# Three edits in one program: GpSimd's order and a subtraction in attention A, an addition in the dense stage, two clamps in attention B

## The reference

```python
x = x + attn_a(_layernorm(x))      # stage "attention A", with its own feed-forward network (first half of "dense")
x = x + ffn(_layernorm(x))         # per group of 1024 rows: two linear maps, no activation between them
x = x + attn_b(_layernorm(x))      # linear attention with memory, segments of 64 rows
x = x + ffn(_layernorm(x))
```

```python
# attn_a, for 16 heads of size 8 and 8 value groups r
score = softmax(einsum('bihd,bjhd->bhij', q, k))
out = einsum('bhij,bjrd->bihrd', score, v)
comp = softmax(concatenate([qv, out]) @ Ws.T + bs, axis=3)   # over r
out = (comp * out).sum(axis=3)
out = res + _lin(out, Wf, bf)                                # "y plus bias": res + bf
# attn_b
sigma(t) = elu(t) + 1       # = max(t, 0) + exp(min(t, 0)), taken of k and of q
```

## Time and profile before

| | us |
|---|---|
| median of 3 runs (1666.82 to 1677.94) | 1674.24 |
| the profiled execution | 1675.07 |
| its span, first to last instruction | 1673.3 |
| TensorE's mean granted clock | 0.962 of full speed |

### The profile page before, as it was taken

How to read it: one execution, slowest core, us unless ns; L and a number is a source line. 1 busy time by engine, 2 the same in 40 slices (tenths; PEclk the granted TensorE clock), 3 DMA queues, 4 the chain that set the end, 5 groups by cost and what they waited for, 6 DMA issues and landing times. The chain is left out here.

```text
span 1673.3 us, 46472 instructions
## 1 busy us (share of the span) xinstructions
PE 1459.9 (87%) x13668; PEld 1242.3 (74%) x13668; DVE 1220.1 (73%) x3362; ACT 869.2 (52%) x2019; POOL 902.9 (54%) x1308
## 2 busy tenths in 40 slices
PE   5899999999999999997587738999999999999986
PEld 3899889898889898897366526766676766667665
DVE  4378888888888888886245446888888888878774
ACT  2466666666666666665366623444444444444431
POOL 4456666666666666664588833444444444444431
PEclk9899999999999999999699958999999999999996
DMA  4423333233333232330444223333333333333330
GB/s 138 147 76 100 94 94 85 78 81 85 94 94 83 78 84 85 91 87 11 118 123 133 84 75 96 102 102 101 107 103 101 108 106 107 107 106 107 98 96 17
DMA packets 181695, 158.10 MB, mean 94 GB/s; under 512 B 12530, under 2 KB 163186, under 8 KB 181619
## 3 DMA queue, kind: packets, MB, share of 16 engines
q1 hardware_dynamic: 181618, 157.17, 32.9%
HBM read 113.09 MB, written 44.04 MB: 94 GB/s over the span
## 5 line engine op out<-in xcount | busy, mean ns | idle before, releaser
L597 PE MATMUL a_bank<-a_vp,a_prob 128*128 128x74 f32 x4096 | 603.6, 253 | 0.0
L597 PEld LDWEIGHTS a_bank<-a_vp,a_prob 128*128 128x128 f32 x4096 | 588.6, 192 | 7.5
L685 DVE TENSOR_REDUCE a_nmax<-a_bank 128x2 f32<-128x512 f32 x512 | 345.7, 681 | 142.9 <-PE a_bank L566 142.0
L484 ACT ACTIVATE a_prob<-a_bank 128x512 f32<-128x512 f32 x512 | 305.4, 596 | 245.8 <-PE a_bank L581 240.5
L581 PE MATMUL a_bank<-a_q_st,a_k_st 120*128 120x256 bf16 x1024 | 281.7, 276 | 27.6 <-POOL a_q_st L345 27.0
L566 PE MATMUL a_bank<-a_k_st,a_q_st 96*128 96x256 bf16 x1024 | 259.9, 277 | 16.9 <-DVE a_nmax L685 12.5
L1627 PE MATMUL c_o_bank<-c_vb,c_prob 128*128 128x96 f32 x1024 | 173.4, 293 | 17.9 <-DVE c_ad L1910 14.0
L1786 DVE TENSOR_REDUCE c_nmax<-c_bank 128x4 f32<-128x512 f32 x256 | 164.8, 684 | 19.7 <-PE c_bank L1597 17.2
L345 POOL TENSOR_SCALAR a_q_st<-a_mt 24x2048 bf16<-24x2048 bf16 x64 | 121.4, 1896 | 103.7 <-PE a_bank L581 60.8
L1492 ACT ACTIVATE c_prob<-c_bank 128x256 f32<-128x256 f32 x256 | 98.8, 386 | 145.8 <-PE c_bank L1577 144.2
L404 POOL TENSOR_TENSOR a_prod<-a_ov,a_wgt 128x512 f32<-128x512 f32 x128 | 151.3, 1182 | 37.3 <-POOL a_prod L404 17.1
(11 more groups left out here) (207 smaller groups left out, 2879.3 us busy)
## 6 DMA issues: line engine op xcount, KB each, us to landing
a_q_st<-scratch_a_parts_dram SPq DMA_DIRECT2D x64, 288.0 KB
a_k_st<-scratch_a_parts_dram SPq DMA_DIRECT2D x192, 96.0 KB
c_q_st<-scratch_c_parts_dram SPq DMA_DIRECT2D x64, 288.0 KB
c_k_st<-scratch_c_parts_dram SPq DMA_DIRECT2D x192, 96.0 KB
scratch_a_parts_dram<-a_parts SPq DMA_DIRECT2D x32, 384.0 KB, 2.7
scratch_c_parts_dram<-c_parts SPq DMA_DIRECT2D x32, 384.0 KB, 2.7
a_x<-in_x SPq DMA_DIRECT2D x32, 128.0 KB, 2.9
scratch_y<-a_y SPq DMA_DIRECT2D x32, 128.0 KB, 2.5
```

Of the source, the lines that this page charges most:

```text
L484: act.activation(prob[h % 4][:, :, :].rearrange("p a b -> p (a b)"), t_ps[h % 2][:, :], ACT.Exp).then_inc(exped, 1)
L597: mm = pe.matmul(o_ps[g % 2][:, at:at + VM], prob[h % 4][:, c, t * P:(t + 1) * P], vp[o][:, c, 0:VM], start=c == 0, stop=c == NT - 1)
L685: dve.tensor_reduce(nmax[:, t, 2 * g:2 * g + 2, 0], s_ps[t][:, :].rearrange("p (h k) -> p h k", h=2), AX.X, ALU.max, negate=True).then_inc ...
```

## The change

In attention A, GpSimd does norm instructions for r1 and the shift first, then the spread of half 0, then the four for r2. The subtraction `comp3 = comp2 - cmax` moves from VectorE's list to GpSimd's, behind the spread of half 1. In dense, y plus bias moves from GpSimd to VectorE, between the moments of x1 and the sum x2. In attention B the two clamps move from VectorE at step 1 to ScalarE at step 2, as Relu of x and Relu of -x; the exponential then takes -neg.

```diff
@@ attention_a, gpsimd body
                 if active(j, u, 2):
                     spread(1, n - 2, i)
+                if active(j, u, 3):
+                    b = n - 3
+                    pool.wait_ge(post, b * POST + 4)
+                    apart(pool, spare)
+                    pool.tensor_tensor(comp3[:, :, :], comp2[:, :, :],
+                                       cmax[:, :].unsqueeze(2).broadcast_to([P, H * NT, R]), ALU.subtract
+                                       ).then_inc(post, 1)
+                    pool.wait_ge(post, b * POST + 5)
...
                     norm(1, pool.tensor_scalar(rt[:, 0, :], mv[:, :, 1], EPS, None, ALU.add))
                     norm(2, pool.tensor_tensor(r1[:, :], rt[:, 0, :], half[:, :], ALU.pow))
-                    norm(3, pool.tensor_tensor(rt[:, 1, :], r1[:, :], r1[:, :], ALU.mult))
-                    norm(4, pool.tensor_tensor(rt[:, 2, :], rt[:, 1, :], mv[:, :, 1], ALU.mult))
-                    norm(5, pool.tensor_scalar(rt[:, 3, :], rt[:, 2, :], EPS, None, ALU.add))
-                    norm(6, pool.tensor_tensor(r2[:, :], rt[:, 3, :], half[:, :], ALU.pow))
-                    norm(7, pool.tensor_scalar(rt[:, 4, :], mv[:, :, 0], -1.0, None, ALU.mult))
-                    norm(8, pool.tensor_tensor(shift[:, :], rt[:, 4, :], r1[:, :], ALU.mult))
+                    norm(3, pool.tensor_scalar(rt[:, 4, :], mv[:, :, 0], -1.0, None, ALU.mult))
+                    norm(4, pool.tensor_tensor(shift[:, :], rt[:, 4, :], r1[:, :], ALU.mult))
                 if active(j, u, 1):
                     spread(0, n - 1, 1 - i)
+                if active(j, u, -1):
+                    apart(pool, spare)
+                    norm(5, pool.tensor_tensor(rt[:, 1, :], r1[:, :], r1[:, :], ALU.mult))
+                    norm(6, pool.tensor_tensor(rt[:, 2, :], rt[:, 1, :], mv[:, :, 1], ALU.mult))
+                    norm(7, pool.tensor_scalar(rt[:, 3, :], rt[:, 2, :], EPS, None, ALU.add))
+                    norm(8, pool.tensor_tensor(r2[:, :], rt[:, 3, :], half[:, :], ALU.pow))
@@ attention_a, vector
-                        lambda: dve.tensor_tensor(comp3[:, :, :], comp2[:, :, :], wide(cmax), ALU.subtract),
+                        None,
...
-                weighs(4, 5)
@@ dense, gpsimd body
-                if has(j, u, 0):
-                    pool.wait_ge(ay_in, (n + 1) * 32)
-                    if later(j, n, 2):
-                        pool.wait_ge(r_d, n - 1)
-                    pool.tensor_tensor(yb[i][:, :, :], y[i][:, :, :], rows(b_f), ALU.add).then_inc(yb_d, 1)
@@ dense, vector body, behind moments(1, n - 2, x1[i])
+                if has(j, u, 0):
+                    if isinstance(j, int) and n == 0:
+                        dve.wait_ge(loaded, N_LOAD * 16)
+                    dve.wait_ge(ay_in, (n + 1) * 32)
+                    if later(j, n, 2):
+                        dve.wait_ge(r_d, n - 1)
+                    dve.tensor_tensor(yb[i][:, :, :], y[i][:, :, :],
+                                      b_f[:, :].unsqueeze(1).broadcast_to([P, C, P]), ALU.add).then_inc(yb_d, 1)
@@ attention_b, scalar body
+                    if s == 2 and active(j, u, 0):
+                        if later(j, n, 1):
+                            act.wait_ge(sg_d, n)
+                        act.activation(flat(pos), ps_a[:, :], ACT.Relu).then_inc(pn_d, 1)
+                        act.activation(flat(neg), ps_a[:, :], ACT.Relu, scale=-1.0).then_inc(pn_d, 1)
...
-                        act.activation(nexp[:, :, :], neg[:, :, :], ACT.Exp).then_inc(nexp_d, 1)
+                        act.activation(nexp[:, :, :], neg[:, :, :], ACT.Exp, scale=-1.0).then_inc(nexp_d, 1)
@@ attention_b, vector body
-                    if s == 1 and active(j, u, 0):
-                        dve.wait_ge(kq_d, (n + 1) * 2)
-                        if later(j, n, 1):
-                            dve.wait_ge(sg_d, n)
-                        dve.tensor_scalar(flat(pos), ps_a[:, :], 0.0, None, ALU.max).then_inc(pn_d, 1)
-                        dve.tensor_scalar(flat(neg), ps_a[:, :], 0.0, None, ALU.min).then_inc(pn_d, 1)
```

More of the change, by code:

```diff
@@ L371, in body, with norm @@
                                                 ALU.subtract))
+                def norm(k, ins):
+                    ins.then_inc(norm_d, 1)
+                    pool.wait_ge(norm_d, (n + 1) * NORM + k)
+                    apart(pool, spare)
                 if active(j, u, -1):
@@ L377, in body @@
                         pool.wait_ge(z_d, (n + 1) * NT)
[L379 to L382, removed]
                     apart(pool, spare)
```

## The result

| | before | after |
|---|---|---|
| median of the runs of one chip, us | 1674.4 (20 runs, 1665.89 to 1679.26) | 1681.6 (20 runs, 1674.61 to 1686.28) |
| ratio, 95% interval | | 1.0044 [1.003, 1.0058] |
| span of the profiled execution, us | 1673.3 | 1679.6 |
| attention A, 31 rounds, us | 717.7 | 700.1 |
| dense, 15 rounds, us | 139.1 | 143.1 |

What follows compares the result with a forecast made beforehand. The prediction took TensorE's matmul order with short waits to bound both attentions, and a ScalarE-TensorE loop the dense stage. A -20, dense +6, B -16.5 made -30.5 from 1675.07: 1644 us, range 1611 to 1690.

Steps and rivals of the forecast that it cites:

- Attention B: Clamps moved to ScalarE: TensorE's waits for VectorE shrink, 0.55 us a block, 16.5 us gained over 30.
- given back: Rival: attention A's gain falls to 9 us and ScalarE's passes make an exponential in B late; 1672 us, chance 0.17.
- Attention A, spread between norm instructions: In attention A, the earlier lower-half spread removes TensorE's wait for it, 0.96 us a block.
- The subtraction: In attention A, moved to GpSimd's idle time, it removes TensorE's wait behind it: 0.25 us a block, bounds 0 and 0.66.
- The meeting: In attention A, later GpSimd products delay VectorE's two weighing steps; of 1.2 us a block 0.70 is left, 20 us.
- The slower rival, weighing meets spread: In attention A, the upper spread holds VectorE's second weighing step: 1.5 us a block more, 1708 us, chance 0.13.
- Dense: VectorE's moved addition holds the norm's first small GpSimd instruction, 0.4 us a unit, +6 us.
- The rival by GpSimd's load: GpSimd's load bounds the dense stage, so losing the addition gives -18 in place of +6: 1621 us, chance 0.08.

Runs made afterwards that it cites:

- only B: Kernel before with only the attention B edit, attention A and dense as before: ratio 1.0108.
- the whole change with the wait: Kernel after, plus GpSimd's addition sg in attention B waiting for VectorE's pair that normalizes z4: ratio 0.9789 to the kernel before, median 1638.98 us.
- only A: Kernel before with only the two attention A edits, dense and attention B as before: ratio 0.9883.
- only dense: Kernel before with only the dense edit, attention A and B as before: ratio 0.9998.

## Why the prediction was wrong

**Attention B is the step that failed**, and in it one thing: what comes behind VectorE's four steps on the maxima. Up to there it held: the cast stretched to 0.60 (forecast 0.5 to 0.7), the wait before the memory matmul gone, ScalarE's two passes 0.62 and 0.63 us and no exponential late, one table load in the page after too, and with the meeting taken away the round is 19.57 to 19.62 for a forecast of 19.6. The prediction summed TensorE's gain to the matmul at line 1698 and let all behind it move forward by the same 0.55. That matmul came as forecast, 0.71 us after GpSimd's last splitting part where it was 1.27. What lies behind it doesn't move together. Count from the end of GpSimd's last splitting part, which is fixed: 1211.12 before, 1202.97 after. The z4 pair starts at +1.75 before, behind VectorE's own list. After, it starts at +1.45, released by GpSimd's small instructions, which stand behind the splitting in GpSimd's list and so can't come earlier. The addition hangs on ScalarE's exponential of `neg`, and that on TensorE, whose wait in front had gone entirely: +2.51 before, +1.52 after. The pair needs 0.60. Before it was through at +2.35, with 0.16 us to spare; after, the addition starts 0.07 us behind the pair's start. The two rows (1212.87 to 1213.47 and 1213.63) were in the trace of before; the prediction names neither. Its rule for GpSimd, that a step moved on an engine may meet its neighbour, was applied in A and in dense, and for the cast in B, but not to what ScalarE's output releases. The price is -0.56 gained and +1.46 lost: +0.90 a round, 21.03 for 20.13.

That the time lies in the stated range is no merit. The rival nearest to it, "given back" (1672), had A's gain falling to 9 us and an exponential in B late; A kept 17.6, and no exponential was late.

The Trainium skill ("SBUF — State Buffer", section "SBUF: two separate sides") says that the SBUF ports which VectorE and GpSimd share are held by one of them for the whole instruction, whichever starts first, and that the other blocks fully. The trace agrees on the size: 1.42 us for the first of the pair is the addition's 1.27 and little more. It differs on who is first: VectorE's record starts at 1204.42, 0.07 us ahead of GpSimd's at 1204.49, and VectorE is the one that waits. The kernels after and "only B" show where the line runs between the records. In all 40 rounds in which GpSimd's starts 0.054 to 0.092 us behind VectorE's, the first of the pair is held (1.40 to 1.44 us). In all 6 in which it starts 0.101 to 0.186 us behind, the first takes 0.35, and only the second is held. One of the six, where the addition in its turn takes 1.36 for 1.27:

```profile
1058.24 1.55 DVE L1774 TENSOR_SCALAR c_z<-c_x,c_mv,c_rs 128x128 f32<-128x128 f32 x2 [0.18 <-POOL c_rs L1412]
```
```profile
1058.35 1.36 POOL L1458 TENSOR_TENSOR c_sg<-c_pos,c_nexp 128x512 f32<-128x512 f32 x1 [0.21 <-ACT c_nexp L1551]
```

**Attention A, spread between norm instructions: right.** The wait for the lower spread went, and the moved instructions made the products late as said. **The subtraction: right in its place, wrong as a term of its own.** It had 0.25 us a block beside 0.96 for the order. The runs show no such split: alone it is worth nothing, and with the new order it adds 7 us to the stage's gain. **The meeting: right.** VectorE's first step runs into the third product, the second into the fourth, 0.60 and 0.83 us. The round is 22.05 for the 22.2 forecast. What was missing is small: in 9 of 26 blocks TensorE waits 0.3 to 1.1 us for the k stack, and those rounds are near 22.95. So the faster loop leaves the transfers little slack, and -17.6 came for -20. The slower rival, weighing meets spread, did not come: the second step's longest in the whole run is 0.84 us, and a spread alone lasts 1.90. Why just these blocks are late was not settled.

By the Trainium skill's rule for two-input elementwise work on GpSimd ("GPSIMD Engine Reference", Engine selection) the subtraction would take about twice its time. Measured are 0.63 us against 0.42 for VectorE unblocked, 1.5 times, and beside the blocked 1.70 it still pays where the new order goes with it.

**Dense: right.** +0.4 a unit came as +0.36, in the instruction that was named. The stage came at +4.0 to +4.6 for +6, since the first units and the last are less than 0.36 longer. The rival by GpSimd's load is excluded by the kernel without the addition, whose unit is 9.32 us and not shorter.

**The end of the run.** In the last interval of B, 11 to 16 us, executions differ by TensorE's granted clock (1.00 is 2.4 GHz, 0.50 is 1.2 GHz, what lies between is a mean of the two). Windows of 10 us, kernel before and the whole change with the wait:

```profile
1643.00:1653.00 10.00, 8.70 (x72) 6.53 (x72) 3.21 (x12) 2.46 (x7) 0.79 (x2) 0.62 0.14 41
1653.00:1663.00 10.00, 7.12 (x45) 5.75 (x45) 3.46 (x10) 1.90 (x5) 0.81 (x2) 0.67 0.04 13
```
```profile
1606.00:1616.00 10.00, 8.70 (x100) 6.93 (x98) 5.94 (x21) 3.25 (x9) 0.00 (x0) 1.00 0.13 39
1616.00:1626.00 10.00, 6.51 (x71) 4.99 (x70) 4.70 (x15) 2.37 (x6) 1.60 (x3) 0.98 0.05 15
```

TensorE is busy 8.70 us of 10 in the first window of both. The last interval is 15.7 us in the one and 11.1 in the other. Long and short ends occur both in kernels that leave B as it was (16.2 in "only A", 11.1 with the order of the norm alone) and in kernels that change it (14.6 in the kernel after, 11.1 in "only B"). So these 4.6 us are not counted for the edits here; whether an edit changes how often the end is long was not tried, nor what sets the clock there. Without that interval the profile of the whole change with the wait has A -17.3, dense +4.4 and B -18.1, -31.0 in all for a forecast of -30.5. That it fits so well is in part luck: A is 2.7 short, and dense and B are 1.6 better each. The end of the run can be why the ratio says -35, and why "only dense" shows no loss in its ratio; only one execution of each kernel was profiled.

## What to carry to other kernels

When an edit takes a wait away, list what is released behind it and by which engine, and measure each from a point that doesn't move: events with different releasers move by different amounts, and a pair that was 0.16 us apart can come to meet. Price that gap for each neighbour of VectorE and GpSimd, not only around the edited instruction. If they do meet, one wait in the right order may be worth more than the edit (here 1.0044 to 0.9789). And judge edits of one loop together: one alone may only uncover the wait that the other removes.

## What the runs showed that I had not expected

A pair of VectorE instructions with one SBUF tensor input of 128 columns is held by GpSimd's two-input instructions, each of the pair by another one: 1.42 us for the first behind the addition of 1.27, the second until the product of 0.73 had ended, 2.10 instead of 0.60. A VectorE instruction whose record starts up to 0.092 us ahead of GpSimd's is still the one that waits; from 0.101 us on it is not. So a few hundredths of a microsecond decide here between 20.45 and 21.03 us a round. GpSimd's small instructions can be held the other way round by VectorE's addition: 0.56 for 0.19, or 1.44 for 1.02.
